# Rows of an expert layer split ahead and turned by a DMA transpose, and its down products as three matmuls of 256 columns

## The reference

```python
xf = layernorm(x).reshape(-1, 256)
top1 = argmax(xf @ gate_w.T + gate_b, axis=-1)          # 8 experts
for e in range(8):
    h = relu(xf @ w1[e].T + b1[e])                       # 256 -> 1024
    y = h @ w2[e].T + b2[e]                              # 1024 -> 256
    out = out + where((top1 == e)[:, None], y, 0)
x = x + out
```

## Time and profile before

| | us |
|---|---|
| median of three runs | 482.56 |
| span of the profiled execution | 492.6 |
| PE busy in it | 402.1 (82%) |
| DVE busy | 346.3 (70%) |
| POOL busy | 208.7 (42%) |
| ACT busy | 177.5 (36%) |
| DMA, mean rate | 141 GB/s |

### The profile page before, as it was taken

How to read it: one execution, slowest core, us unless ns; L and a number is a source line. 1 busy time by engine, 2 the same in 40 slices (tenths; PEclk the granted TensorE clock), 3 DMA queues, 4 the chain that set the end, 5 groups by cost and what they waited for, 6 DMA issues and landing times.

```text
span 492.6 us, 16316 instructions
## 1 busy us (share of the span) xinstructions
PE 402.1 (82%) x5967; PEld 338.3 (69%) x5967; DVE 346.3 (70%) x777; ACT 177.5 (36%) x317; POOL 208.7 (42%) x213
## 2 busy tenths in 40 slices
PE   0135868888888866897999999779999999999992
PEld 0025757887787765896887877557778877877871
DVE  7978969789945863477757877457666666766662
ACT  3343255542624221342434433224333333433420
POOL 8345374334673467523723242642333323233221
PEclk9999999999999999975699999889999999999998
DMA  8999578899685664377612232544333322222210
GB/s 282 414 305 218 135 170 241 212 259 260 160 220 119 152 167 107 106 173 181 207 45 67 68 76 81 185 131 155 90 68 77 77 62 62 69 60 61 84 31 0
DMA packets 105162, 69.39 MB, mean 141 GB/s; under 512 B 78077, under 2 KB 88190, under 8 KB 104576
## 3 DMA queue, kind: packets, MB, share of 16 engines
q1 hardware_dynamic: 75696, 56.67, 41.9%
q10 hardware_dynamic: 25984, 3.21, 4.6%
q0 software_dynamic: 3408, 8.46, 4.6%
HBM read 48.28 MB, written 12.57 MB: 124 GB/s over the span
## 4 chain that ended last, share of the span: by engine, by line
PE 55%; DMA 11%; SPq 9%; DVE 9%; issue 6%; POOL 5%; ACT 2%; ACTq 1%; another core or an unknown queue 1%; POOLq 0%; DVEq 0%
PE s_ps L1229 20%; SPq L305 8%; PE at_ps L1245 6%; DMA arena<-qv_hl 6%; PE pv_ps L1245 6%; PE pv_ps L1143 6%; PE s_ps L1111 3%; PE lg_ps L1171 3%; PE pv_ps L1246 3%; PE at_ps L1246 3%; POOL qv_hl L987 2%; PE tr_ps L1156 2%; DMA arena<-x 2%; PE st_ps L1196 2%; POOL k_hl L995 1%
## 5 line engine op out<-in xcount | busy, mean ns | idle before, releaser
L1229 PEld LDWEIGHTS s_ps<-arena 128*128 x1872 | 132.7, 99 | 52.2 <-issue 14.6
L1229 PE MATMUL s_ps<-arena 128*128 128x128 f16 x1872 | 158.6, 222 | 8.4 <-DVE arena L906 5.1
L915 DVE SCALAR_TENSOR_TENSOR arena<-arena,s_ps 128x512 f32<-128x512 f32 x78 | 53.6, 687 | 48.6 <-PE s_ps L1229 35.9
L1076 POOL DMA_INDIRECT result<-arena x39 | 38.8, 995 | 95.5 <-DVE arena L940 91.6
L1111 PEld LDWEIGHTS s_ps<-k_hl,arena 128*128 128x128 f16 x1536 | 54.3, 118 | 29.9 <-DMA arena<-qv_hl 22.1
L1111 PE MATMUL s_ps<-k_hl,arena 128*128 128x16 f16 x1536 | 54.7, 179 | 23.3 <-DMA arena<-qv_hl 19.3
L1143 PE MATMUL pv_ps<-a_hl,arena 128*128 128x16 f16 x1536 | 54.7, 179 | 19.7 <-DMA arena<-qv_hl 15.9
L1143 PEld LDWEIGHTS pv_ps<-a_hl,arena 128*128 128x128 f16 x1536 | 53.5, 118 | 22.8 <-DMA arena<-qv_hl 18.3
L1245 PE MATMUL at_ps<-arena,k_in 128*128 x160 | 60.9, 383 | 0.8 <-DVE k_hl L926 0.6
L1245 PE MATMUL pv_ps<-arena,x_in 128*128 x152 | 58.1, 383 | 0.1
L1069 POOL TENSOR_TENSOR arena<-arena 128x256 f32<-128x256 f32 x39 | 30.7, 786 | 60.7 <-DMA arena<-b 60.6
(11 more groups left out here) (143 smaller groups left out, 614.2 us busy)
## 6 DMA issues: line engine op xcount, KB each, us to landing
arena<-w SPq DMA_DIRECT2D x28, 512.0 KB, 6.1
arena<-sorted_rows SPq DMA_DIRECT2D x39, 130.0 KB, 2.4
arena<-b SPq DMA_DIRECT2D x39, 128.0 KB
arena<-qv_hl SPq DMA_DIRECT2D x70, 64.0 KB, 3.5
k_in<-k_t SPq DMA_DIRECT2D x16, 256.0 KB, 3.9
v_in<-v_t SPq DMA_DIRECT2D x16, 256.0 KB
arena<-x SPq DMA_DIRECT2D x4, 1024.0 KB, 12.1
o_sb<-x_r SPq DMA_DIRECT2D x16, 256.0 KB, 3.8
```

What stands on the lines that cost most here:

```text
L915: eng.scalar_tensor_tensor(out=h_in[:, c].rearrange("p (k t) -> p k t", t=P), in0=bias, scalar=W_SCALE, in1=h_ps[c][:].rearrange("p (k t) ...
L1076: eng.indirect_dma_start(out=out, out_offset=bass.IndirectOffsetOnAxis(ap=rows[:, r, :].bitcast(I32)[:, D + 2:D + 3], axis=0), in_=rows[:, ...
L1229: k = eng.matmul(o, weights_of(j, w + k_ * H + n * P, P), xt[:, j % 2, k_ * P:(k_ + 1) * P], start=k_ == 0 and w is HI_1 and xt is xt_hi, ...
```

## The change

Four things are changed, and the table of due times is shifted.

1. PE no longer transposes. ACT casts `xn2` to its upper part and DVE subtracts for the lower one, both before the transpose, into `x2_hl` (512 half-precision columns, two buffers). SP then issues one DMA transpose per tile from `x2_hl` to `xt` (three buffers), and the ups wait for its landing.
2. Normalizing, cast and subtraction are due some 5.7 us, one tile, earlier than before; the fetch of rows is 6.2 us earlier. The loads of the biases are a loop of their own.
3. The downs are three matmuls of 256 columns per unit instead of one of 512 and one of 256, all into the same half of a bank. DVE then adds the result in one operation.
4. The rows that fill up each expert's last tile are written in 8 DMAs instead of 12 (the last with five times the bytes), the router's last group of rows is due 5.7 us earlier, and the last turned outputs of the attention 2.5 us earlier. `h_in` moves to another part of SBUF.

```diff
-        xt_hi = carve(q_flat, 2 * D).rearrange("p (n c) -> p n c", n=2)
-        xt_lo = carve(q_flat, 2 * D).rearrange("p (n c) -> p n c", n=2)
+        x2_hl = carve(q_flat, 4 * D).rearrange("p (n c) -> p n c", n=2)
+        xt = carve(q_flat, XB * 2 * D).rearrange("p (n c t) -> p n c t", n=XB, t=P)
...
@@ SP
+            def turn_rows():
+                for j in range(NTILES):
+                    yield tile_at(j) - 2.9
+                    sp.wait_ge(s_x2_hi, j + 1)
+                    sp.wait_ge(s_x2_lo, j + 1)
+                    sp.wait_ge(s_up, 2 * (j - XB + 1))
+                    eng.dma_start_transpose(xt[:, j % XB], x2_hl[:, j % 2]).then_inc(s_xt[j % XB], 16)
...
@@ ACT
-                    yield tile_at(j)
+                    yield tile_at(j) - 5.7
                     act.wait_ge(s_rows[r], 16 * (j // FR + 1))
-                    act.wait_ge(s_xt2, j)
+                    act.wait_ge(s_x2_lo, j)
                     eng.activation(xn2, rows[:, r, 0:D], ACT.Identity, ...
-                    yield tile_at(j) + 1.5
-                    act.wait_ge(s_xt2, j + 1)
-                    act.wait_ge(s_up, 2 * (j - 1))
-                    eng.copy(xt_hi[:, j % 2], xt2_ps).then_inc(s_xt_hi, 1)
+                    yield tile_at(j) - 5.6
+                    act.wait_ge(s_xn2, j + 1)
+                    if j >= 2:
+                        act.wait_ge(s_xt[(j - 2) % XB], 16 * ((j - 2) // XB + 1))
+                    eng.copy(x2_hl[:, j % 2, 0:D], xn2).then_inc(s_x2_hi, 1)
@@ DVE
-                    yield tile_at(j) + 2.0
-                    dve.wait_ge(s_xt_hi, j + 1)
-                    dve.wait_ge(s_up, 2 * (j - 1))
-                    eng.tensor_tensor(xt_lo[:, j % 2], xt2_ps, xt_hi[:, j % 2], ALU.subtract).then_inc(s_xt_lo, 1)
+                    yield tile_at(j) - 3.7
+                    dve.wait_ge(s_x2_hi, j + 1)
+                    eng.tensor_tensor(x2_hl[:, j % 2, D:2 * D], xn2, x2_hl[:, j % 2, 0:D], ALU.subtract).then_inc(s_x2_lo, 1)
...
-                    for n in range(2):
-                        yield tile_at(j) + 14.4 + 0.5 * n
...
-                            out=y, in0=y_ps[j % 2][:, n * D:(n + 1) * D], scalar=1.0 / (W_SCALE * W_SCALE), in1=y,
-                            op0=ALU.mult, op1=ALU.add).then_inc(s_y, 1)
+                    yield tile_at(j) + 14.4
...
+                        out=y, in0=y_ps[j % 2][:, 0:D], scalar=1.0 / (W_SCALE * W_SCALE), in1=y,
+                        op0=ALU.mult, op1=ALU.add).then_inc(s_y, 1)
@@ PE
-                    for k_ in range(KD):
-                        k = eng.transpose(xt2_ps[:, k_ * P:(k_ + 1) * P], xn2[:, k_ * P:(k_ + 1) * P], ident[:])
-                    k.then_inc(s_xt2, 1)
...
-                            pe.wait_ge(s_xt_lo, j + 1)
-                            pe.wait_ge(s_xt_hi, j + 1)
+                            pe.wait_ge(s_xt[j % XB], 16 * (j // XB + 1))
...
                         at = BOTH_2 + 2 * n * D
-                        eng.matmul(y[:], h_hi[j % 2][:, n * P:(n + 1) * P], weights_of(j, at, 2 * D), start=n == 0, stop=False)
-                        k = eng.matmul(y[:, 0:D], h_lo[j % 2][:, n * P:(n + 1) * P], weights_of(j, at, D), start=False,
-                                       stop=n == KH - 1)
+                        for a, h, w in ((0, h_hi, at), (1, h_hi, at + D), (2, h_lo, at)):
+                            k = eng.matmul(y, h[j % 2][:, n * P:(n + 1) * P], weights_of(j, w, D), start=(n, a) == (0, 0),
+                                           stop=(n, a) == (KH - 1, 2))
```

## The result

The changed kernel takes **501.1 us** (median of 4 runs, 498.3 to 502.8) where the kernel before takes 483.6 on the same chip: a ratio of **1.041** (95% interval 1.035 to 1.046). The prediction was 499.3, with a range of 473.5 to 509. Some executions of one and the same kernel come out a few per cent longer; the ratios in this document leave those out, while each time is a median over all runs, so that the times don't always divide to the ratio beside them.

The account below looks back on a forecast made before the run. PE's array was taken to bound the kernel before, its sequencer the kernel after. Terms 10.5 + 2.4 + 3 + 2 - 0.4 - 0.8 = +16.7 us on 482.6 gave 499.3, with a range of 473.5 to 509.

Parts of the forecast that it names:

- The bound moves to the sequencer: In each tile PE's sequencer would need 6.14 us, more than the array's 5.30, and set the period; chance 0.60.
- The price of an addition: On PE's sequencer, eight more register additions per tile at about 0.12 us each would cost 0.95 us.
- The rival of the array with 0.032 us per addition: Additions cost only their recorded duration, PE stays bound by its array at about 5.35 us per tile: 473.5 us, chance 0.20.
- the one at 0.06: Half hidden rival: an addition costs about 0.06 us more, the period stays near 5.7 us: 484 us, chance 0.12.
- The array's 5.30: PE's array per tile: 5.51 us less 0.23 for the transposes plus 0.02 for the ninth matmuls makes 5.30.
- From 355 us on, +10.5, and 264 to 286 us, +2.4: Longer tiles: 21 from 355 us on at 6.19 us for 5.69, and four at 6.14 for 5.53.
- The middle, +3 (0 to 6), with the fetch's -0.8: 286 to 355 us: ten tiles' additions partly swallowed by stalls, +3; earlier fetches and fills shorten ACT's wait for rows, -0.8.
- Up to 264 us, +2 (0 to 5): Before 264 us: DVE's subtraction of tile 0 and SP's first transpose hold up other work, and a few additions show, +2.
- The tail: At the very end, DVE's two result operations of 0.42 us become one, -0.4 us.
- The transfer hidden: SP's transpose would land in 3 to 4 us, within 6.2 free; the late-transpose rival (9 us) gave 551, chance 0.08.
- How the timeline would look: PE: period 6.1 to 6.2 us, gap of 0.6 to 0.8 at tile heads, units 0.67 to 0.68, additions at 0.12.
- The +16.7: Sum of all terms over the profiled span, 492.6 to 509.3 us, put unscaled on the median of 482.6 to give 499.3.

Follow-up runs that it names:

- the kernel with four additions: The changed kernel with all three down products' weights at fixed addresses, 4 register additions per unit for 6; 479.1 us beside 479.9 of the kernel before.
- the two of 5.28: The changed kernel with its old downs put back (ratio 0.965 to the kernel before), and with only each unit's second down product's weights at a fixed address (0.981).
- the wide downs: The changed kernel with downs put back to one matmul of 512 columns and one of 256, transfer kept; 479.3 us beside 497.5 of the kernel before.
- the new downs alone: The kernel before with only the downs changed to three products of 256 columns, PE still transposing; 515.6 us beside 500.4, ratio 1.026.
- the one with one more address: The kernel before with each unit's 256-column down reading its weights at another address, one more register addition per unit; 512.9 us beside 500.4, ratio 1.029.

## Why the prediction was right, point by point

**The bound moves to the sequencer.** Right, and shown from both sides: eight additions without a matmul cost what the change costs (6.29 us per tile), nine matmuls without them cost nothing (5.28).

**The price of an addition.** Taken as 0.95 us for eight, from the distance in the earlier trace rows and not from the recorded 0.032. Measured: 0.96 from 47 to 55. The rival of the array with 0.032 us per addition is excluded, and so is the one at 0.06. Every addition that was tried is followed by an instruction that reads its result; whether one that nothing reads would cost as much was not tried. The 5.19 us of the sequencer's own work, from one wait in the earlier trace rows, was good too: with 39 additions and nobody to wait for, an ordinary tile takes 5.20.

**The array's 5.30.** Right: 5.30 in the kernel with four additions, and nothing against it in the two of 5.28. That the saving would be lost under the sequencer was right too; with the sequencer relieved it comes back, as the wide downs show.

**From 355 us on, +10.5, and 264 to 286 us, +2.4.** Measured +10.7 and +2.6.

**The middle, +3 (0 to 6), with the fetch's -0.8.** Wrong in the profile: -4.5 beside the first profile of before, outside its bounds, and +1.4 on another chip. The +3 for the additions themselves was good. The ten tiles from 7 to 17 take 68.8 us before, and 72.4 and 72.8 us in the two kernels that take little more than the additions from the change, the new downs alone and the one with one more address:

```profile
L1203 PEldq FUSED_REGOPS  x11: 141/198/208, 295.2 to 367.6; - x11
...
L1207 PEldq FUSED_REGOPS  x11: 141/197/208, 300.2 to 373.0; - x11
```

That is +3.6 to +4.0 us, so that the stalls swallow some of the additions and not all. But the whole change takes 64.3 us for the same tiles, and 68.7 on the other chip. The step that failed is that the sum takes off nothing there but the 0.8 for fetches and fills: the rest of the change, the rows turned a tile ahead and the moved due times, gives 4 to 8 us back (a rough figure, since it is taken across chips; the kernel before took 67.3 us there on the second one). The stall ahead of tile 11 was a wait for DVE's lower part of that same tile, and this is what the change takes a tile earlier. Which of the two, the lead or the due times, does it was not tried.

**Up to 264 us, +2 (0 to 5).** -0.5 in the first profile and +4.1 in the one on another chip, where the first tile's head comes at 246.9 for 240.4. Nothing sizes the term: the first head lies between 239.9 and 241.3 us in the first two profiles and in all from the chip where the kernel before takes 479.9, and on the two others it moves between 237.3 and 252.6 from one profile to the next.

**The tail.** 0 for -0.4.

**The transfer hidden.** Right, with more room than was thought. Tile 21's transfer is issued at 370.5 us, lands 2.46 us later where 3 to 4 were taken, and the head comes at 377.1: 6.6 us were free where 6.2 were taken. From tile 22 on there is room for a second one. In the middle, landings of up to 5.9 us came close to the limit, which the prediction did not look at.

**How the timeline would look.** Partly: additions, distances and the 51 ns of the waits are as written (though the 51 ns can't show what they were named for), but the gap is not 0.6 to 0.8 us at the tile's head; it is spread over the units, which take 0.67 to 0.91 us.

**From the profile to the median.** The +16.7 was put on the median because no part seemed to scale with the 10 us by which the profiled execution was longer. The timed difference is +17.5, so this held, but not through the terms as written: the same terms add up to +8.3 between the two profiles, so that the nearness of 499.3 to 501.1 is in part luck. The range was 35 us wide and reached from a gain to the loss; what was right by more than luck is the period. The profile of the change is as long as its timed runs, the first profile of before was 10 us longer than its own. Its three tiles from the stall on are 9.8 us over ordinary ones. On which chip it was taken is not on record. That the timed runs beside the change have no such stall, so that the middle costs them some +5 rather than -4.5, would fit; no profile of a short run of before exists, so it stays open. The same holds for the ratio, 1.04 where the kernel before takes 480 to 484 us and 1.029 where it takes 497.

**What the faster version is worth.** The wide downs with the transfer beat both kernels by their interval (0.965 of the kernel before), on the two chips on which the kernel before takes 497 to 500 us. It was not run on a chip where the kernel before takes 480. There the kernel with four additions, of the same period of 5.3 us, took 479.1 us in its one run beside 479.9, so that the gain may be smaller or none on such a chip.

## What to carry to other kernels

Before an instruction is split into more instructions with addresses from registers, count the operands whose address must be computed and take the distance between two such register operations, not their recorded duration: eight additions were 0.95 us of a 5.5 us tile, the matmul that they served cost nothing. PE's busy share can't show this bound, and neither can the recorded durations of the waits; look at the distances between the sequencer's own rows, with no gap that a semaphore explains, while the array's units start late. And a part of a change that is hidden in the steady stretch can matter where other work is routed: one stretch, one sum.

## What the runs showed of the hardware

- A register addition on PE's sequencer between matmuls is recorded with 32 ns and costs 0.12 us of its time, the same from 39 to 47 and from 47 to 55 per tile (5.20, 6.16 and 7.09 us for an ordinary tile), with or without another matmul that goes with it.
- The sequencer and the array overlap well: at 39 additions (5.20 us, and 5.8 to 6.0 in one tile of eight) and 5.3 us of array work the period is 5.28, and at 31 it is 5.30. What was handed out ahead bridges the longer tile: PE is busy for 84.50 of 84.50 us.
- A wait of PE's sequencer can be recorded with 51 ns however long it was: nine rows of 51 ns stand in a stretch where the heads of tiles 11 to 15 came 7.2 us late in all.
- A transposing transfer of 128 x 512 elements of two bytes inside SBUF holds SP for 1.23 us to issue it, and lands 2.4 us after the start of the issue at the least, 2.46 at tile 21, up to 4.3 in the steady tiles and up to 5.9 while the last group is routed. Two of them per 6.2 us tile, 2.5 us of SP, changed nothing where SP had little else to do, and cost 7.4 us over 15 tiles where it also fills and fetches.
- The same program took 479.9 us on one chip and 497.5 to 500.4 on two others.
